# Matmuls with unread results on TensorE ahead of, and between, the first row scores of an attention block

## The reference, cut to what matters

```
xn = _ln(x, g1, b1)
q = _lin(xn, Wq, bq).reshape(b, n, H, HD) / sqrt(HD)
k = _lin(xn, Wk, bk).reshape(b, n, H, HD)
score = softmax(einsum('bihd,bjhd->bhij', q, k), axis=-1)
v = _lin(xn, Wv, bv).reshape(b, n, R, HD)
out = einsum('bhij,bjrd->bihrd', score, v)
```

## Time and profile before

| | |
|---|---|
| median of 3 runs | 1225.6 us (1223.35 to 1225.65) |
| profiled execution: span from the first to the last instruction | 1220.2 us |
| profiled execution: time | not given apart from its span; the median of the runs is 5.4 us above the span |
| TensorE busy | 1168.7 us (96%) |
| VectorE, GpSimd, ScalarE busy | 951.7 us (78%), 956.5 us (78%), 756.2 us (62%) |
| chain of work that ended last, by engine | TensorE 83%, VectorE 8% |
| mean granted clock of TensorE | 0.985 of full speed |

### The profile page before, as it was taken

One profiled execution on the slowest core, in us unless ns is written; L12 is line 12 of the kernel. 1 busy time (PEld: TensorE's weight loads), 2 busy tenths in 40 slices (PEclk: granted clock), 3 DMA queues, 4 the chain that ended last, 5 costly groups with the idle time before them and its releaser, 6 DMA issues.

```text
span 1220.2 us, 27563 instructions
## 1 busy us (share of the span) xinstructions
PE 1168.7 (96%) x7997; PEld 541.7 (44%) x7997; DVE 951.7 (78%) x2127; ACT 756.2 (62%) x1461; POOL 956.5 (78%) x561
## 2 busy tenths in 40 slices
PE   4699999999999999999999999999999999997898
PEld 2144444444444444444444444444444444435675
DVE  7676788888888787878788888788888878768762
ACT  4066766666666766666666676666666666664443
POOL 5277898989898898988898989898888878883321
PEclk9599999999999999999999999999999999999999
DMA  5334444344444443444444344544344434330000
GB/s 128 109 66 92 100 96 106 79 107 97 110 90 100 94 94 84 101 101 90 100 96 105 84 105 95 111 98 98 85 92 93 93 83 98 73 71 18 18 26 26
DMA packets 55765, 107.14 MB, mean 88 GB/s; under 512 B 6144, under 2 KB 25056, under 8 KB 55728
## 3 DMA queue, kind: packets, MB, share of 16 engines
q0 software_dynamic: 18784, 67.70, 29.3%
q1 hardware_dynamic: 36162, 38.65, 10.1%
q10 hardware_dynamic: 782, 0.33, 0.1%
HBM read 22.51 MB, written 8.39 MB: 25 GB/s over the span
## 4 chain that ended last, share of the span: by engine, by line
PE 83%; DVE 8%; issue 4%; DMA 2%; POOL 1%; ACT 1%; DVEq 1%; SPq 0%; POOLq 0%; ACTq 0%
PE out_bank L1077 33%; PE row_bank L1048 17%; PE col_bank L1067 17%; PE den_bank L917 5%; DVE rowmax L1242 3%; PE turn_bank L926 2%; PE down_bank L1501 2%; DVE att_all L389 2%; DMA q_op<-max_rows 1%; PE turn_bank L254 1%; PE mid_bank L1521 1%; PE den_bank L934 1%; POOL norm_rstd L576 1%; DVE norm_normed L584 0%; PE out_bank L1491 0%
## 5 line engine op out<-in xcount | busy, mean ns | idle before, releaser
L1242 DVE TENSOR_REDUCE rowmax<-row_bank 128x1 f32<-128x512 f32 x1024 | 662.7, 685 | 184.5 <-PE row_bank L1048 180.3
L1192 ACT ACTIVATE prob<-col_bank 128x512 f32<-128x512 f32 x1024 | 554.7, 594 | 263.6 <-PE col_bank L1067 261.9
L1077 PE MATMUL out_bank<-prob,v_op 128*64 128x512 f32 x2048 | 534.4, 594 | 0.2 <-ACT prob L1192 0.2
L1351 POOL TENSOR_TENSOR addend<-prob 128x1024 f32<-128x1024 f32 x128 | 323.4, 2526 | 45.6 <-ACT prob L1192 45.6
L1351 POOL TENSOR_TENSOR quad<-prob 128x1024 f32<-128x1024 f32 x128 | 335.5, 2621 | 20.4 <-ACT prob L1192 20.2
L1048 PE MATMUL row_bank<-k_op,q_op 72*64 72x512 bf16 x2048 | 327.0, 387 | 13.5 <-DMA q_op<-q_parts 9.0
L1067 PE MATMUL col_bank<-q_op,k_op 74*64 74x512 bf16 x2048 | 317.2, 382 | 3.1 <-DMA q_op<-max_rows 2.0
L1067 PEld LDWEIGHTS col_bank<-q_op,k_op 74*64 74x64 bf16 x2048 | 118.1, 109 | 246.2 <-ACT prob L1192 208.3
L1048 PEld LDWEIGHTS row_bank<-k_op,q_op 72*64 72x64 bf16 x2048 | 122.6, 109 | 153.4 <-DVE rowmax L1242 55.2
L1077 PEld LDWEIGHTS out_bank<-prob,v_op 128*64 128x64 f32 x2048 | 152.9, 136 | 67.3 <-issue 8.3
L1356 POOL DMA_DIRECT2D quad<-addend x128 | 112.7, 880 | 77.5 <-POOL addend L1351 72.9
(11 more groups left out here) (201 smaller groups left out, 805.9 us busy)
## 6 DMA issues: line engine op xcount, KB each, us to landing
quad<-addend POOLq DMA_DIRECT2D x128, 512.0 KB, 5.3
k_op<-k_parts SPq DMA_DIRECT2D x64, 144.0 KB
q_op<-q_parts SPq DMA_DIRECT2D x192, 48.0 KB
v_op<-v_all SPq DMA_DIRECT2D x32, 256.0 KB, 5.9
q_parts<-along_parts SPq DMA_DIRECT2D x11, 192.0 KB, 2.1
k_parts<-along_parts SPq DMA_DIRECT2D x33, 64.0 KB, 2.1
out<-y_out SPq DMA_DIRECT2D x8, 256.0 KB, 2.3
q_op<-max_rows SPq DMA_DIRECT2D x64, 4.0 KB
```

The costliest lines, as they stand in the source:

```text
L1077: last = nc.tensor.matmul(out_bank[ih * VW:(ih + 1) * VW, :], v_op[slot // 2][:, t, :], outs.halves(prob[:, t, :])[:, :, ih, :], start=(t ...
L1192: nc.scalar.activation(prob[:, t, h * HALF:(h + 1) * HALF], col_bank[h][:, :], ACT.Exp).then_inc(exp_done, 1)
L1242: nc.vector.tensor_reduce(rowmax[:, parity, t, h:h + 1], row_bank[h][:, :], AX.X, ALU.max).then_inc(max_done, 1)
L1351: pool.tensor_tensor(dst, prob[:, 2 * k, :], prob[:, 2 * k + 1, :], ALU.add).then_inc(pair_done, 1)
```

## The change

In `prepare`, ScalarE waits for the first tiles of `x` and copies four of them three times, into `words` (float32r), `plain_words` (float32) and `short_words` (bfloat16), ahead of `colsT`. TensorE, after the turn of `wf_n`, waits for the last values to be read and for these copies, and runs `keep_running()`: 32 matmuls of 512 columns into banks whose contents have been read, ahead of the barrier. In `attention`, `between(t)` puts four matmuls of the row scores' own shape behind each of the 12 steps of the lead; they write `out_bank`, which `values` later starts afresh. No result of an added matmul is read.

```diff
+        words, plain_words, short_words = (sb("words", [P, HALF], WORD), sb("plain_words", [P, HALF]),
+                                           sb("short_words", [P, HALF], BF16))
...
+            act.wait_ge(x_in[0], DMA)
+            for kept in (words, plain_words, short_words):
+                nc.scalar.activation(kept[:, :], res.x[:, 0:BLOCK_TILES, :].rearrange("p t d -> p (t d)"),
+                                     ACT.Copy).then_inc(words_ready, 1)
             act.wait_ge(cols_turned, 1)
...
+            def unused(to, rows, cols, dtype):
+
+                source = {WORD: words[:, :], FP32: plain_words[:, :], BF16: short_words[:, :]}[dtype]
+                nc.tensor.matmul(bank[to][cols, :], source[rows, 0:cols.stop - cols.start], source[rows, :],
+                                 start=True, stop=True)
+
+            def keep_running():
+
+                all_, half, word = slice(0, P), COLUMN_TILES, WORD
+                for n in range(4):
+                    unused(n, all_, all_, word)
+                for n in range(4):
+                    for k in range(2):
+                        unused(2 * (n % 2) + k, half[k], all_, word)
+                for n in range(3):
+                    for c in range(2):
+                        for k in range(2):
+                            unused(2 * (n % 2) + k, half[k], half[c], BF16)
+                for c in range(2):
+                    unused(4, all_, half[c], FP32)
+                for n in range(2):
+                    for k in range(2):
+                        unused(2 * n + k, half[k], all_, word)
+                for c in range(2):
+                    unused(5, all_, half[c], FP32)
...
             nc.tensor.transpose(bank[6][:, 2 * DIM:3 * DIM], wf_n[:, :], res.identf[:, :]).then_inc(wf_turned, 1)
+            pe.wait_ge(project.v_ready, PAIRS_BEFORE)
+            pe.wait_ge(words_ready, 3)
+            keep_running()
...
             pe.wait_ge(operands_in[0], LOADS * DMA)
+            def between(t):
+
+                for c in range(2):
+                    for h in range(2):
+                        nc.tensor.matmul(out_bank[c * VW:(c + 1) * VW, :], q_op[0][0:PROD_ROWS, c * VW:(c + 1) * VW],
+                                         k_op[0][0:PROD_ROWS, h * HALF:(h + 1) * HALF], start=True, stop=True)
+
             for t in range(TB):
                 row_scores(0, 0, t, t == 0)
+                between(t)
             pe.wait_ge(operands_in[1], LOADS * DMA)
             for t in range(LEAD - TB):
                 row_scores(1, 1, t, False)
+                between(t)
```

More of the change, by code:

```diff
@@ L23 @@
 BF16 = mybir.dt.bfloat16
+WORD = mybir.dt.float32r
 ALU = mybir.AluOpType
@@ L672, in prepare @@
                                                          sem("proj_ready"))
+        words_ready = sem("words_ready")
         qsb_ready, wf_turned, wf_copied = sem("qsb_ready"), sem("wf_turned"), sem("wf_copied")
```

## The result

Over twelve executions the changed kernel has a median of 1226.2 us (1223.6 to 1226.9), the kernel before, over twelve of its own, 1222.95 us (1221.3 to 1227.3). One of the twelve executions of the changed kernel took 3643.6 us, for no cause on record, and is left out of the range and of the ratio. The ratio is 1.0020, 95% interval 1.0011 to 1.0030: **slower by 0.2%, about 2.5 us** (the medians lie 3.25 us apart). The forecast was 4.8 us faster; rival 1 had the sign and most of the mechanism. In the profiled execution (1225.1 us, 1.8 above its span) the span is 3.1 us longer than before.

The account below looks back on a forecast made before the run. TensorE, busy in 96% of the span, was taken to bound the kernel, partly at a slow clock. Terms -2.15 and -2.65 made -4.8 us; with 0.1 given back, 1220.9 us, 0.38% less, range 1218.8 to 1228.8.

Parts of the forecast that it names:

- rival 1: Clock falls in the gap before the operands, lead runs dense at 1.2 GHz: +3.4 us, 1229.0 us, slower; chance 0.17.
- The lead at 2.4 GHz: Row-score steps before group 0 shrink from 1.43 to 1.21 us, less 0.43 for the last added matmuls: net -2.15 us.
- the start of group 0: First column scores to values of the third step, at 2.4 GHz: 5.7 us instead of 8.32, -2.65 us.
- The three copies: ScalarE's copies in `prepare`, at most 1.9 us, fit in idle time before `colsT`: cost 0.
- The list: The 32 matmuls before the barrier: 9.0 us at 1.2 GHz, ending between 38 and 39.5 us; cost 0.
- The number called weakest: Time of each float32r turn in the list before the barrier: taken as 0.43 us, as bfloat16, not 1.71.
- The first rise: During the matmuls ahead of the barrier, the clock rises to 2.4 GHz between 34.5 and 37.5 us.
- The sum of -4.8: Whole kernel: -2.15 in the lead and -2.65 at the start of group 0; 0.1 us was then given back.
- Rival 2: Clock falls before the lead, but dense work there raises it again after 6.4 us: 1222.7 us; chance 0.09.
- Rival 3: Clock swings in the lead, half the steps at either level: -1.9 to +0.8 us, middle 1225.1 us; chance 0.10.
- Rival 4: In the list before the barrier, float32r takes float32's time, row scores 3.7 us late: 1224.5 us; chance 0.07.
- The range: Whole kernel's time forecast between 1218.8 and 1228.8 us, leaving out half of rival 1 and a little at the bottom.

Follow-up runs that it names:

- experiment 3: Changed kernel plus eight unread bfloat16 matmuls (128 rows, 128 columns) behind the barrier, filling the gap before the row scores; ratio 1.0003 to the kernel before.
- 11: Changed kernel with its 48 lead matmuls reading 128 rows of a resident tile instead of 72, gap left open; ratio 0.9967 to the kernel before.
- experiment 4: Changed kernel with two full 128-row, 128-column matmuls per lead step instead of four over 72 rows, gap open; ratio 1.0019 to the kernel before, two groups.
- experiment 9: Changed kernel without the list ahead of the barrier, four 128-row matmuls behind each lead step, no fill; ratio 0.9976 to the kernel before.
- experiment 2: Changed kernel with only the 32 matmuls ahead of the barrier and the copies, nothing added in the lead; ratio 1.0000 to the kernel before.
- experiment 6: Changed kernel with lead matmuls reading 128 rows instead of 72 and eight full matmuls filling the gap; ratio 0.9964 to the kernel before.
- 8: Changed kernel with 128-row lead matmuls, nine fill matmuls and the list without its last six; ratio 0.9960, median 1218.1 against 1223.5 us for the kernel before.
- experiment 1: Changed kernel with only the 48 lead matmuls over 72 rows; list ahead of the barrier and copies removed; ratio 1.0029 to the kernel before.
- 12: Changed kernel with lead matmuls reading 72 rows of a resident bfloat16 tile of x, gap open; ratio 1.0020 to the kernel before.
- experiment 10: Changed kernel without the list ahead of the barrier, two full undivided-array matmuls behind each lead step; ratio 1.0046 to the kernel before.
- experiment 5: Changed kernel with eight full matmuls filling the gap and two full undivided-array matmuls behind each lead step; ratio 0.9975 to the kernel before.

## Why the prediction was wrong

The step that failed is *The lead at 2.4 GHz*: it took the clock to stay up "if the gap of 2 to 3.3 us to them does not bring it down", and TensorE's 71% of work in the lead as enough to keep it. Row scores did start on time (41.11) and at 2.4 GHz. But behind a gap of 2.0 us the clock fell 1.9 us into the lead, and the lead became 2.9 us longer in place of 2.15 shorter, the start of group 0 0.3 us shorter in place of 2.65. What came in its place is rival 1, which had 0.17: steps of 1.71 us at 1.2 GHz. The rival held the clock to be lost by idle time alone. The runs show that this is only a part: with the gap filled the clock fell all the same, 12.4 us on (experiment 3), and with 128 rows at work it held behind open gaps of 0.6 and 1.0 us (11, 4) and rose by itself where there was no list (9). I treated every matmul as the same work for the clock. The trace of before had the sign of it: 3.4 us of dense matmuls over 72 and 74 rows at the head of group 0 left the clock at 0.50, and it rose at 64.9 only after the first values, over 128 rows, had run. I wrote this down for rival 1 and did not draw on it for the forecast.

Point by point:

- *The three copies, cost 0.* Right: in the changed kernel they run from 5.71 to 7.38 us, and ScalarE then waits 5.7 us for the first operand of `colsT`; the kernel that has the copies and the list alone has a ratio of 1.0000 (experiment 2).
- *The list, 9.0 us at 1.2 GHz, ending between 38 and 39.5.* Right: it ended at 39.1 and the barrier came at 39.3 instead of 38.6. The number called weakest was right at 1.2 GHz. In experiment 4 the clock was low for the whole of the first eight turns, four full matmuls and four pairs of row halves:

```profile
32.86 4.08 PE L794 MATMUL prep<-words 128*128 128x512 f32 x12
36.86 1.34 PE L794 MATMUL prep<-short_words 64*64 64x512 bf16 x12
```

They take 4.00 us. Inside this row two full matmuls or two pairs in a row start 0.43 us apart (33.45, 33.87 and 34.30 for the full ones), the 0.43 taken; the rest, 0.13 to 0.16 us each time, lies behind the first of either form and ahead of the next form, which I had left out. The two pairs that ran at 2.4 GHz, between other forms, took 0.33 us each in the changed kernel (37.40 to 38.06), where 0.21 was counted. (In the profiled executions of experiments 3 and 4 the clock rose later and the barrier with the same list came at 41.2 and 41.1.)

- *The first rise.* Right: at 36.2, within 34.5 to 37.5, though the clock had been up until 32.8 and not fallen at 30.7 as before.
- *The lead at 2.4 GHz, -2.15.* The mechanism exists, once the clock is held: 15.32 us against 17.18 is -1.86 (experiments 6, 8, 11). The first eight steps of experiment 6 take (54.47 - 44.66) / 8 = 1.23 us each, as forecast 1.21. Most of the rest is the split of the maxima ahead of the turn: VectorE's four small operations stand between the maxima at either clock, and the step that holds them, the ninth, takes 1.78 us (54.47 to 56.25) where before it took 1.79 (52.83 to 54.62). It saved nothing, and I had counted 0.22 for it.
- *The start of group 0, -2.65.* 5.90 against 8.32, -2.42 (forecast 5.7).
- *The sum of -4.8* stands, for a kernel whose clock holds, at -4.3 in the profiled stretches and -4.1 to -5.4 us in the medians (experiments 8 and 11: 1218.1 against 1223.5, 1219.5 against 1223.7). The changed kernel does not reach it. Worked out without rounding, the two terms of the sum are -2.2 and -2.6 and not -2.15 and -2.65, which changes nothing.
- *Rival 1's size.* +3.4 for a lead wholly at 1.2 GHz; experiment 1 has +3.36 in the lead. The changed kernel keeps 1.9 us at 2.4 GHz and loses 2.9.
- *Rival 2*, that the dense lead raises the clock again, is excluded for 72 rows by experiment 1 and is what happens for 128 (experiment 9).
- *Rival 3*, the swing: the clock of none of the profiled leads went down and up again; what the page named there describes is not what happened.
- *Rival 4*, float32r at the time of float32: excluded by the rows on the list above.
- *The range* (1218.8 to 1228.8) holds the 1226.2, but partly by luck. Its base of 1225.6 was a median of three, 2.65 us above the 1222.95 of twelve, and the 5.4 us added to the span set that median against one profiled execution; in the changed kernel time and span of the same execution are 1.8 apart. From 1222.95 the forecast would have been 1218.3, and rival 1, stated as 1229.0 and thus above the range, 1226.35.

Still open: how long a gap the clock stands with each kind of work. In the profiled executions with 128 rows in the lead gaps were 1.0 us (experiment 4) and 0.6 us (11), with 72 rows 2.0 us (the changed kernel) and 2.3 us (12). A gap of 2 us followed by 128 rows was not caught in a profile. No number of rows between 72 and 128 was tried, and none of the runs says why rows matter. And the seven executions of experiment 4 above 1227 us fit what experiment 10 shows, that full matmuls in an undivided array don't bring a lost clock back.

## What to carry to other kernels

To keep TensorE's clock up with unread matmuls, use the whole height of the array, and the same division into columns as the work around them (with matmuls over the undivided array in between, the changes cost time and a clock that was low did not rise); the same count of 72-row matmuls only put their own 0.85 us per step on the path. Read from the profile which kind of work had been running when the clock last rose, not only how busy the engine was. Matmuls that were meant to be free at the fast clock have to be priced at the slow one too: here 48 added matmuls come with 4 to 5 us less where the clock holds, and with 2.5 to 3.5 us more where it does not.

## What the hardware showed that was not expected

- TensorE, busy for 20.5 of 20.5 us with bfloat16 matmuls over 72 rows and 64 columns (two side by side), stayed at 1.2 GHz (experiment 1); with every second four over 128 rows it rose after 4.9 us (experiment 9). With 128 rows the clock also held through pauses, 13.0 us busy of 15.3 (experiment 6).
- Alternating between an array divided into column halves and an undivided one cost 0.13 us per change at 1.2 GHz (1.96 against 1.71 us for a step with two changes), and the clock, low at the start, did not rise in 23.5 us (experiment 10). Where it was up, it stayed up (experiment 5).
- At 1.2 GHz a float32r matmul of 512 columns over the undivided array, or a pair over its row halves, took what bfloat16 takes, 0.43 us (experiment 4). At each change between full matmuls and pairs of row halves 0.13 to 0.16 us came on top. What a pair takes in a row of its own kind at 2.4 GHz no run shows.
